# Mixing weights of all batches by eight matmuls at the start, kept in DRAM, and weight-block differences begun behind the first route

## The reference, cut to what matters

```python
h = gelu(cond @ W0 + b0); h = gelu(h @ W1 + b1)
att = softmax(h @ W2 + b2)                       # [64 batches, K = 8]
agg_w = einsum('bk,koi->boi', att, weight)       # one 64x64 mixing matrix for each batch
agg_b = att @ bias_k
c = einsum('boi,bih->boh', agg_w, x) + agg_b[:, :, None]
out = c @ W.T + b                                # 1024 x 1024
scores = c @ gate_w.T + gate_b                   # 4 ranks, the best one is taken
lora = [c @ A[:r].T @ B[:, :r].T for r in (8, 16, 32, 64)]
x = x + out + lora[argmax(scores)]
```

## Time and profile before

| | |
|---|---|
| time, median of 3 runs | 473.72 us (472.91 to 475.15) |
| time of the profiled execution | 473.84 us |
| its span, first to last instruction | 472.0 us |
| outside the span | 1.8 us |
| PE / DVE / ACT / POOL busy | 453.1 / 338.3 / 170.1 / 124.1 us |
| mean granted TensorE clock | 0.994 |

### The profile page before, as it was taken

How to read it: one execution, slowest core, us unless ns; L and a number is a source line. 1 busy time by engine, 2 the same in 40 slices (tenths; PEclk the granted TensorE clock), 3 DMA queues, 4 the chain that set the end, 5 groups by cost and what they waited for, 6 DMA issues and landing times.

```text
span 472.0 us, 8555 instructions
## 1 busy us (share of the span) xinstructions
PE 453.1 (96%) x2703; PEld 448.4 (95%) x2703; DVE 338.3 (72%) x741; ACT 170.1 (36%) x366; POOL 124.1 (26%) x112
## 2 busy tenths in 40 slices
PE   6977799999999999999999999999999999999996
PEld 5867699999999999999999999999999999999996
DVE  5499998667768676676777667676867677677634
ACT  6543542433324343323424343332434333342411
POOL 1079703205050311405040220505031140504000
PEclk9998999999999999999999999999999999999999
DMA  8930170331607042250705134070614316070202
GB/s 246 341 146 23 70 240 28 136 134 31 238 2 255 12 177 90 68 198 0 266 1 204 63 117 150 12 254 0 218 49 160 107 52 215 0 267 2 91 0 90
DMA packets 18114, 56.09 MB, mean 119 GB/s; under 512 B 2465, under 2 KB 4785, under 8 KB 18098
## 3 DMA queue, kind: packets, MB, share of 16 engines
q1 hardware_dynamic: 17954, 55.83, 33.9%
q10 hardware_dynamic: 144, 0.07, 0.1%
HBM read 39.04 MB, written 16.83 MB: 118 GB/s over the span
## 4 chain that ended last, share of the span: by engine, by line
PE 89%; DVE 8%; DMA 1%; issue 1%; SPq 0%; ACT 0%; DVEq 0%
PE p_r L851 53%; PE p_ab L851 19%; PE p_o L866 3%; PE p_o L867 3%; PE p_o L868 3%; PE p_o L885 3%; PE p_o L884 3%; DVE wbl L611 1%; DVE bd L654 1%; DMA b2r<-in_b 1%; DVE wbl L620 1%; PE p_u L873 1%; DVE prod L645 1%; DVE xl L632 1%; PE p_o L897 1%
## 5 line engine op out<-in xcount | busy, mean ns | idle before, releaser
L851 PE MATMUL p_r<-wch,xh 128*128 128x364 f32 x256 | 85.1, 332 | 1.1 <-DVE xl L752 0.7
L851 PE MATMUL p_r<-wcl,xh 128*128 128x364 f32 x256 | 85.1, 332 | 0.3 <-DVE wcl L604 0.3
L851 PE MATMUL p_r<-wch,xl 128*128 128x364 f32 x256 | 85.0, 332 | 0.0
L851 PE MATMUL p_r<-wbh,xh 128*128 128x364 f32 x252 | 83.9, 333 | 0.0
L851 PE MATMUL p_r<-wbl,xh 128*128 128x364 f32 x252 | 83.0, 329 | 0.0
L851 PE MATMUL p_r<-wbh,xl 128*128 128x364 f32 x252 | 82.7, 328 | 0.0
L391 POOL TENSOR_TENSOR ubias<-bias,gbias 128x136 f32<-128x136 f32 x16 | 10.0, 622 | 230.5 <-DVE usplit L703 230.4
L851 PE MATMUL p_ab<-wbh,xh 128*128 128x364 f32 x192 | 63.4, 330 | 0.0
L851 PE MATMUL p_ab<-wbh,xl 128*128 128x364 f32 x192 | 63.3, 330 | 0.0
L851 PE MATMUL p_ab<-wbl,xh 128*128 128x364 f32 x192 | 63.1, 328 | 0.0
L632 DVE TENSOR_TENSOR xl<-raw,xh 128x512 fp32r<-128x512 f32 x60 | 53.6, 895 | 0.8 <-ACT xh L486 0.4
(11 more groups left out here) (147 smaller groups left out, 820.5 us busy)
## 6 DMA issues: line engine op xcount, KB each, us to landing
xin<-in_x SPq DMA_DIRECT2D x32, 512.0 KB, 4.1
raw<-in_xt SPq DMA_DIRECT2D x31, 512.0 KB, 4.4
out<-xin SPq DMA_DIRECT2D x30, 512.0 KB, 4.1
wb_raw<-in_wb SPq DMA_DIRECT2D x8, 364.0 KB, 7.6
wc_raw<-in_wc SPq DMA_DIRECT2D x8, 182.0 KB, 3.7
out<-xin SPq DMA_DIRECT2D x4, 182.0 KB, 2.0
xin<-in_bt SPq DMA_DIRECT2D x2, 256.0 KB, 9.3
raw<-in_xt SPq DMA_DIRECT2D x1, 384.0 KB, 4.1
```

What stands on the lines that cost most here:

```text
L851: last = nc.tensor.matmul(o, a[:, n, cols], w, start=start and p == 0, stop=stop and p == 2, skip_group_check=True)
```

## The change

All 64 mixing matrices are made at the start by TensorE: `kernels` comes as 128 x 256 numbers, is split on DVE into `kern_h` and `kern_l`, written to DRAM (`g_kern`) and read back as rows (`k_rows`, 8 kernels by 4096 numbers, three times: high, low, high, at partitions 0, 32 and 64). The transposed attention rows (`att_rows`, high, high, low) times `k_rows` in eight chunks of 512 columns gives `aggw` of all batches. ACT copies the chunks out to `aggw_all`, SP stores them to DRAM (`g_aggw`) and loads for each pair the 64 KB that it needs. `mixing_weights` on DVE goes away, with `attp`, `attd`, `own` and `ones`. `k_rows` and `aggw_all` lie where `xin` lies, so the loads of `b`, `bt`, `x` and of pair 1's `xt`, which stand behind them in SP's list, now come after the stores.

On POOL `u_bias(0, 1)` moves ahead of the eight `t_sum`, so that these begin behind the first `route`. The splits of T1 and T3 (`t_hi`, `t_lo`) move into `step(0, 1)`, and TensorE waits for T2, T1, T3 apart. On DVE and ACT some operations of pair 0 change places.

```diff
@@ sync
                     sp.dma_start(bk[:, :], bias_k).then_inc(s_bk_in, 16)
+                    sp.dma_start(kern[:, :], kernels).then_inc(s_kern_in, 16)
...
-                if n == 0:
-                    for h in (slice(0, C), slice(C, P)):
-                        sp.dma_start(kern[h, :, :], kernels).then_inc(s_kern_in, 16)
             sp.dma_start(gbias[:, R:RE], gate_b.partition_broadcast(P)).then_inc(s_gate_in, 16)
+            def mixing_weights(i, j):
+                if not is_pair(i, j, 0):
+                    sp.wait_ge(s_bdl, count(i, j, 2, 0))
+                sp.dma_start(aggw[:, :, :], g_aggw_pair[i * 2 + j]).then_inc(s_aggw_in, 16)
+            for n in range(KCH):
+                sp.wait_ge(s_aggw_ev, n + 1)
+                sp.dma_start(g_aggw.rearrange("b i o -> b (i o)")[:, n * BANK:(n + 1) * BANK],
+                             aggw_all[:, n * BANK:(n + 1) * BANK]).then_inc(s_aggw_stored, 16)
+            sp.wait_ge(s_aggw_stored, 16 * KCH)
+            mixing_weights(0, 0)
             sp.dma_start(brow[:, :], b.rearrange("(a o) -> a o", a=1)).then_inc(s_brow_in, 16)
...
             gate_rows(0, 0)
+            mixing_weights(0, 1)
             sp.wait_ge(s_b_hi, 1)
@@ gpsimd
+            nc.gpsimd.memset(k_rows[:, :].bitcast(F32), 0.0).then_inc(s_clear, 1)
             def u_bias(i, j):
+                if not is_pair(i, j, 0):
+                    pool.wait_ge(s_ubias, count(i, j, 1, 0))
...
             u_bias(0, 0)
-            pool.wait_ge(s_bl, 6)
+            u_bias(0, 1)
+            pool.wait_ge(s_bl, 8)
...
-            u_bias(0, 1)
             s_sums(0, 1)
@@ scalar
-            for k in range(2, KC):
+            for k in range(2, KC - 1):
                 wc_hi(k)
+            act.wait_ge(s_kern_hl, 2)
+            for n, rows in enumerate((kern_h, kern_l)):
+                act.dma_start(g_kern[n].rearrange("k (a n) -> (k a) n", n=K * C * C // P),
+                              rows[:, :].bitcast(F32)).then_inc(s_k_stored, 16)
+            wc_hi(KC - 1)
             act.wait_ge(s_raw_in[1], 16)
 ...
+            act.wait_ge(s_clear, 4)
+            act.wait_ge(s_k_stored, 16 * 2)
+            for row, n in ((K_HI, 0), (K_LO, 1), (K_HI2, 0)):
+                act.dma_start(k_rows[row:row + K, :].bitcast(F32), g_kern[n]).then_inc(s_k_rows, 16)
             wb_hi(0, R11, wbh[:, B11, :, :])
             wb_hi(1, R21, wbh[:, B21, :, :])
+            for n in range(KCH):
+                act.wait_ge(s_aggw_mm, n + 1)
+                nc.scalar.activation(aggw_all[:, n * BANK:(n + 1) * BANK], ps_aggw[n % 2], ACT.Copy).then_inc(s_aggw_ev, 1)
             cs_hi(0)
             z_hi(0, 0, C1)
             wb_hi(2, R12, b12h[:, :, :])
-            bd_hi(0, 0, 0)
             wb_hi(3, R22, wbh[:, B22, :, :])
             z_hi(0, 0, C2)
+            bd_hi(0, 0, 0)
             bd_hi(0, 0, 1)
+            cs_hi(1)
+            z_hi(0, 0, Z11)
...
@@ vector
+            for row in (K_HI, K_LO):
+                last = nc.vector.tensor_copy(att_hl[:, row:row + K].bitcast(F32R), att[:, :])
+            wc_lo(3)
+            nc.vector.tensor_tensor(att_hl[:, K_HI2:K_ROWS], att[:, :], att_hl[:, 0:K], ALU.subtract).then_inc(s_att_hl, 1)
+            dve.wait_ge(s_kern_in, 16)
+            nc.vector.tensor_copy(kern_h[:, :], kern[:, :]).then_inc(s_kern_hl, 1)
+            wc_lo(4)
+            nc.vector.tensor_tensor(kern_l[:, :], kern[:, :], kern_h[:, :].bitcast(F32), ALU.subtract).then_inc(s_kern_hl, 1)
...
-            mixing_weights(0, 0, 0)
             z_lo(0, 0, C1)
             wb_lo(2, R12, b12h[:, :, :], b12l[:, :, :])
-            mixing_weights(0, 0, 1)
             wb_lo(3, R22, wbh[:, B22, :, :], wbl[:, B22, :, :])
+            z_lo(0, 0, C2)
             bd_lo(0, 0, 0)
-            z_lo(0, 0, C2)
             bd_lo(0, 0, 1)
+            cs_lo(1)
+            z_lo(0, 0, Z11)
+            route(0, 0)
             dve.wait_ge(s_b_hi, 1)
             nc.vector.tensor_tensor(b_l[:, :], brow[:, :], b_h[:, :].bitcast(F32), ALU.subtract).then_inc(s_b_lo, 1)
-            t_lo(R11, T1)
-            t_lo(R12, T3)
-            mixing_weights(0, 1, 0)
-            mixing_weights(0, 1, 1)
@@ vector, step
                 z_lo(i, j, C1)
+                if is_pair(i, j, 1):
+                    t_lo(R11, T1)
+                    t_lo(R12, T3)
                 s_lo(i, j, S3)
                 s_lo(i, j, S4)
-                if not last:
-                    mixing_weights(i, j + 1, 0)
-                    mixing_weights(i, j + 1, 1)
@@ tensor
+            def mixing_chunk(n):
+                if n >= 2:
+                    pe.wait_ge(s_aggw_ev, n - 1)
+                nc.tensor.matmul(ps_aggw[n % 2], att_rows[:, :], k_rows[0:K_ROWS, n * BANK:(n + 1) * BANK],
+                                 start=True, stop=True).then_inc(s_aggw_mm, 1)
...
             for k in range(KC):
                 done = term(r1, A21 + k // KH, k % KH, wch[:, k, :], wcl[:, k, :], k == 0, k == KC - 1)
+                if k == 0:
...
+                    pe.wait_ge(s_att_rows, 1)
+                    pe.wait_ge(s_k_rows, 16 * 3)
+                else:
+                    mixing_chunk(k - 1)
+            mixing_chunk(KCH - 1)
             done.then_inc(s_z, 1)
+            pe.wait_ge(s_aggw_ev, KCH)
```

More of the change, by code:

```diff
@@ L94, in adaln_ffn @@
         R11, R12, R22, R21 = range(4)
-        xin = sb("xin", [P, 4, H])
+        xin = place("xin", [P, 4, H], F32, at_xin)
+        k_rows = place("k_rows", [P, C * C], F32R, at_xin)
+        aggw_all = place("aggw_all", [NB, C * C], F32, at_xin)
         raw = sb("raw", [P, 2, H])
@@ L114, in adaln_ffn @@
         bias = sb("bias", [P, 2, RE])
-        kern = sb("kern", [P, C, K])
-        attp = sb("attp", [P, T, K])
-        prod = sb("prod", [P, C, K])
+        kern = sb("kern", [P, K * C * C // P])
+        kern_h = sb("kern_h", [P, K * C * C // P], F32R)
+        kern_l = sb("kern_l", [P, K * C * C // P], F32R)
+        att_hl = sb("att_hl", [NB, K_ROWS])
+        att_rows = sb("att_rows", [K_ROWS, NB], F32R)
         aggw = sb("aggw", [P, 2, C])
@@ L353, in step @@
                 if not last:
+                    mixing_weights(i, j + 1)
+                if not last:
                     for t in range(2):
@@ L640, in s_lo @@
                                         ALU.subtract).then_inc(s_sl, 1)
-            def mixing_weights(i, j, t):
-                if not (is_pair(i, j, 0) and t == 0):
-                    dve.wait_ge(s_aggw, count(i, j, 2, t))
-                nc.vector.tensor_tensor(prod[:, :, :], kern[:, :, :],
-                                        attp[:, i * 4 + (2 * j + t), :].unsqueeze(1).broadcast_to([P, C, K]),
-                                        ALU.mult).then_inc(s_prod, 1)
-                dve.wait_ge(s_prod, count(i, j, 2, t + 1))
-                nc.vector.reduce_sum(aggw[:, t, :], prod[:, :, :], AX_X).then_inc(s_aggw, 1)
             def bd_lo(i, j, t):
@@ L708, in _ @@
             nc.vector.memset(warm[:, :], 0.0).then_inc(s_sm, 1)
-            nc.vector.memset(ones[:, :], 1.0)
             first = slice(0, FIRST * P)
@@ L754, in _ @@
             wb_lo(0, R11, wbh[:, B11, :, :], wbl[:, B11, :, :])
-            dve.wait_ge(s_cond_mm, 6)
-            nc.vector.tensor_copy(attp[:, :, :].rearrange("p t k -> p (t k)"), ps_attp).then_inc(s_attp, 1)
+            cs_lo(0)
+            wb_lo(1, R21, wbh[:, B21, :, :], wbl[:, B21, :, :])
+            dve.wait_ge(s_cond_mm, 4)
             nc.vector.tensor_copy(aggb[:, :, :].rearrange("p a t -> p (a t)"), ps_aggb).then_inc(s_aggb, 1)
@@ L779, in _ @@
                                     ALU.subtract).then_inc(s_bt_lo, 1)
-            route(0, 0)
-            cs_lo(2)
             z_lo(0, 0, Z22)
-            t_lo(R11, T1)
-            t_lo(R12, T3)
-            mixing_weights(0, 1, 0)
-            mixing_weights(0, 1, 1)
             a_lo(0, 1, A11)
             a_lo(0, 1, A12)
+            z_lo(0, 0, Z12)
             residual(0, 0, C1)
             residual(0, 0, C2)
-            z_lo(0, 0, Z12)
             residual(0, 0, Z11)
@@ L920, in _ @@
                 done = term(r1, A21 + k // KH, k % KH, wch[:, k, :], wcl[:, k, :], k == 0, k == KC - 1)
[L921 to L935 removed]
+                if k == 0:
+                    pe.wait_ge(s_attt, 1)
+                    pe.wait_ge(s_bk_in, 16)
+                    for d in range(2):
+                        nc.tensor.matmul(ps_aggb[d * C:(d + 1) * C, :], bk[:, :], attt[:, d, :], start=True, stop=True)
+                    for d in range(2):
+                        last = nc.tensor.matmul(ps_aggbt[:, d * C:(d + 1) * C], attt[:, d, :], bk[:, :],
+                                                start=True, stop=True)
+                    last.then_inc(s_cond_mm, 1)
+                    pe.wait_ge(s_att_rows, 1)
[3 more added lines that the diff above has]
+            mixing_chunk(KCH - 1)
+            done.then_inc(s_z, 1)
+            pe.wait_ge(s_aggw_ev, KCH)
```

(2 more changed lines are left out.)

118 lines of the change are left out of this document (56 added, 62 removed).

## The result

The changed kernel takes 487.24 us (487.08 to 488.04, 4 runs) against 474.38 us (472.91 to 475.15, 4 runs) of the kernel before on the same chip: ratio 1.028, 95% interval 1.025 to 1.031. It is slower, as forecast, but by 12.9 us where 6.9 were worked out, and its time lies outside the range. The profiled execution has a span of 485.2 us, 13.2 more than before.

A forecast was written before the change was run, and what follows sets the result against it. PE hides DVE's work in the steady loop; its early waits, all ending on DVE, decide the time. T 4.2 us later plus 2.7 us more to mix(0, 1, C1) made 6.9, from 473.84 to 480.7, stated as 480.5; range 474.0 to 486.0.

The forecast's parts named there:

- the first term: Start of the kernel: the chain of splits, stores and loads until k_rows has landed, put at 23.5 us.
- K: The moment k_rows has landed for PE, forecast at 23.5 us, with 18 and 31 as the ends.
- the third sum: The adding up from T to mix(0, 1, C1): route, ubias, differences, four sums, then DVE's list, ending at T + 32.3.
- The wait and its clock: PE's stall for k_rows, 5.9 us, plus 1.6 for half clock; from K to T 15.6 without the clock.
- T: Start of mix(0, 0, C1) on PE, 36.50 us before the change; forecast 40.7, which is 4.2 later.
- The clock behind it: Low clock after PE's stall of some 5 us before mix(0, 1, C1): 1.6 us added.
- Few partitions are slow: Rival, chance 0.18: load speed goes with partitions reached, so k_rows lands at 26.5, three us more; 483.5 us.
- the third term: From T to mix(0, 1, C1) on PE: T + 33.9 with the clock in place of T + 31.2, 2.7 us more.
- The matrices' trip is late: Rival, chance 0.10: the mixing matrices' two DRAM trips take 5.0 us each, bd_lo is 3 us behind PE; 483.5 us.
- k_rows is early: Rival, chance 0.20: both landings near 2 us, k_rows there at 18.5, no half clock, T about 35; 475 us.
- It is faster: Rival, chance 0.12: POOL runs undisturbed, mix(0, 1, C1) starts at T + 29.5; 470.6 us with early K.
- The point that decides: In the faster rival: with T below 38.2 us the kernel gets faster.

The follow-up runs named there:

- e4: The changed kernel with the last four of eight weight loads on SP's queue held until k_rows has landed; 487.1 us (one run).
- e7: The changed kernel with k_rows loaded into every fourth partition in place of eight neighbours, attention rows laid out to match; 484.8 us (one run).
- e12: The changed kernel with k_rows on every fourth partition and the last four weight loads held until k_rows has landed; 483.3 us, ratio 1.019.
- e2: The kernel before with only POOL's differences begun behind the first route and the T1, T3 splits moved; mixing weights stay on DVE; 474.4 us, ratio 1.001.
- e3: The changed kernel with kernels loaded once straight into eight rows of k_rows, unsplit, chunks as plain fp32 matmuls; 491.9 us, ratio 1.038.
- e1: The changed kernel with POOL's eight differences made right behind the first ubias again, as before the change; 486.8 us, ratio 1.029.

## Why the prediction was wrong

The direction, the places and the order of events were right. The failed step is the first term, the moment K, and in it the two landings that were chosen between bounds; a second, smaller one is a term of the third sum.

- **K: 27.9 in place of 23.5.** The kernels are split at 12.43 (12.2) and the second store is issued at 12.82 (12.7). *"The weight loads are still under way, but on the other queue, so I take 3.5"*: the landing was 6.63, above even the upper end of 5.0. The reason given, the other queue, did not hold: with half of the weights held (e4) it is 4.93. That is 3.1 of the 4.4 us. *"The nearest row is kern, the same 128 KB ... I take 6.5"*: 7.50. The size matched, the shape did not, and the number was near by luck, since spread over more partitions the same load takes 3.12 (e7). That is 1.0; issues make up the rest.
- **The wait and its clock.** PE waited 10.5 us in place of 5.9. From K to T it took 17.4 us, against 15.6 + 1.6 = 17.2: this term held here, in part by luck, since behind the shorter waits of e7 and e12 it was 17.8 and 18.1. The trip of the matrices was hidden as said: they came at K + 13.6 in place of K + 11.8, and `bd_lo(0, 0, 0)` still ended 1.2 us ahead of PE, so T had no wait of its own. So T is 8.8 us later in place of 4.2.
- **T to mix(0, 1, C1): 33.8 in place of 32.3.** The route ends at 50.03, T + 4.7 (4.6). *"ubias 0.5"* is the term that failed: it took 1.45, where DVE had started the 1x1024 low part of `b` 0.12 us ahead of it. In e2, where that low part stands ahead of the route, it took 0.48. `ubias` ends at T + 6.3 (5.1), the differences at T + 22.8 (21.5), with 16.47 us for the eight (16.4), the fourth sum at T + 28.3 (27.1), and `z_lo` at T + 33.8 (32.3). So 1.2 of the 1.5 us are there from `ubias` on. Behind the fourth sum, 6.05 less 0.7 makes 5.35 and not the 5.2 of the prediction; it measured 5.45. PE's own waits were not as said, 4.0 us on the way in place of 2.5 and 4.0 before the mix in place of 5, but the mix goes by DVE's path and not by them.
- **The clock behind it**: 1.6 was said, 1.5 came.
- **The steady loop** is unchanged, as said: G moves with the span.

In sum 4.6 + 1.5 - 0.1 = 6.0 us were missing up to G, 12.87 against 6.9. e12 bears most of this out, but not to the us: with K at 22.8 the time is 483.3, where the split would give 481.6 (480.7, less 0.7 for K, and 1.6 for the rest). The clock's share grew there, as told above.

**The rivals.** *Few partitions are slow* was given 0.18 and is what happens. The Trainium skill, "SBUF — State Buffer", "The DMA port swizzle", says that bandwidth depends on how many of 16 ports the partitions reach; by it eight neighbours reach two ports, and eight partitions at a distance of four reach eight. The runs agree in direction: 7.50 us from the last issue to the landing with the narrow rows, 3.12 with the spread ones, and the same again in e4 (7.43) and e12 (3.17). They don't give the factor of four: less the 1.8 us of the small transfer it is 4.4 counted from the last issue and 2.1 counted from the first (8.37 and 4.98). The rival's price, 8 + 1.8 us behind the stores, is right within 1.4 (8.4 measured from the first issue). Its 483.5 was too low because it kept the store's 3.5 and the third term's 2.7. *The matrices' trip is late*: no. *k_rows is early* and *It is faster* fell with K, and the second of them with its distance too: it needed 29.5 us from T to C1, and in e2, e3, e4, e7 and e12, which keep the order of the change there, it was 33.6 to 33.8. The point that decides, T below 38.2, was never reached in a run with the weights on TensorE (40.9 at best, e12), so it stays untested there; with the measured distance of 33.8 in place of 29.5 it would lie near 33.9 (67.73 less 33.8), an estimate.

## What to carry to other kernels

A load that TensorE will wait for is priced by its partitions and by what else is in flight, not by its bytes and its queue alone; where the trace has no row of its shape, take the upper end. Work taken from an engine that the steady loop does not wait for is worth nothing there, while a new chain in front of the first product costs all by which it is longer than the work that it runs beside. And a gain at the head of an in-order list is kept only if nothing put behind it stands ahead of the next thing that TensorE needs: the same reordering was no faster than the kernel before (ratio 1.003) or 0.8% faster, by where the split of T4, that of A12 and one pair's mixing weights stood.

## What the runs showed of the hardware

- The granted clock fell to the lower of its two levels, 1.2 GHz, with PE busy for 2.00 of 2.00 us in each window from 20 to 38 us, while fp32 matmuls of 8 rows stood between the passes of C2 (e3: 1.00 until 24, 0.62 from 24 to 26, 0.50 behind that). Idle time in the profile is not the only thing that goes ahead of a fall.
- Three loads of 128 KB into eight neighbouring partitions each: data until 25, landing at 27.9 (and until 23 and 25.99 in e4). Into spread partitions: data until 24, landing at 24.96. That the last microseconds are data waiting to be written is a guess; the trace doesn't show it.
- Spreading makes the issue dearer: three issues take 1.86 us on ACT from the first issue to the last (19.98 to 21.84) in place of 0.87 (19.53 to 20.40).
- Beside POOL's 128x728 subtraction a 64x64 one on DVE took 1.66 us in place of 0.22 (e1). The other way round, a 128x136 addition on POOL took 1.45 us in place of 0.48 where DVE's 1x1024 one had started ahead of it.
